# Four attention groups with a set-up each become one bulk projection and one loop of 16 sequences, and the transposed scores go one row group at a time

## What is computed

```python
x = x + tanh(g_xattn[0]) * L0_xattn(layernorm(x), ctx)   # 16 heads of 8 features, softmax over 120 keys, output projection
x = x + tanh(g_ffn[0])   * L0_ffn(layernorm(x))          # 16 experts, gates of the best 4 of each row, clipped sigmoid-gated units
x = x + tanh(g_xattn[1]) * L1_xattn(layernorm(x), ctx)   # one head of 128 features
x = x + tanh(g_ffn[1])   * L1_ffn(layernorm(x))          # 128 -> 512, 9 butterfly stages, gelu, 9 butterfly stages, 512 -> 128
```

## Time and profile before

| | us |
|---|---|
| three runs, median (lowest, highest) | 579.15 (575.86, 581.64) |
| the profiled execution, own time | 580.77 |
| its span, first to last instruction | 578.9 |
| PE busy | 448.4 (77%) |
| DVE busy | 354.1 (61%) |
| POOL busy | 264.3 (46%) |
| ACT busy | 226.5 (39%) |
| mean granted TensorE clock | 0.853 |

### The profile page before, as it was taken

How to read it: one execution, slowest core, us unless ns; L and a number is a source line. 1 busy time by engine, 2 the same in 40 slices (tenths; PEclk the granted TensorE clock), 3 DMA queues, 4 the chain that set the end, 5 groups by cost and what they waited for, 6 DMA issues and landing times. The chain is left out here.

```text
span 578.9 us, 8643 instructions
## 1 busy us (share of the span) xinstructions
PE 448.4 (77%) x2977; PEld 301.6 (52%) x2977; DVE 354.1 (61%) x849; ACT 226.5 (39%) x409; POOL 264.3 (46%) x286
## 2 busy tenths in 40 slices
PE   0347967885798579834999895999869998957785
PEld 0336746663676467623565453555445554524455
DVE  0755543562463346334779999789977998674321
ACT  1112321322123112323566764576537655725421
POOL 8999954980799552000334335234422434240000
PEclk9999976985986588655599998899969997997889
DMA  7112102200431220020000000000000000000001
GB/s 218 39 54 75 37 1 91 70 6 5 142 117 43 72 72 1 0 73 0 1 0 1 2 1 0 1 1 1 0 0 0 0 1 1 1 0 0 19 19 36
DMA packets 13440, 17.38 MB, mean 30 GB/s; under 512 B 1840, under 2 KB 9954, under 8 KB 13412
## 3 DMA queue, kind: packets, MB, share of 16 engines
q1 hardware_dynamic: 9804, 12.98, 7.0%
q10 hardware_dynamic: 3032, 1.96, 1.3%
q0 software_dynamic: 576, 2.10, 1.1%
HBM read 15.98 MB, written 1.05 MB: 29 GB/s over the span
## 5 line engine op out<-in xcount | busy, mean ns | idle before, releaser
L358 POOL TENSOR_TENSOR rings<-rings 128x512 f32<-128x512 f32 x32 | 42.3, 1322 | 98.7 <-DVE rings L1234 91.8
L771 PE MATMUL bank<-xhl,w_hi 128*128 128x512 f32 (+1 forms) x128 | 79.8, 624 | 0.0
L507 ACT ACTIVATE rings<-bank,b1c 128x512 f32<-128x512 f32 x64 | 44.1, 689 | 76.1 <-PE bank L773 45.6
L358 POOL TENSOR_TENSOR wide<-rings 128x512 f32<-128x512 f32 x32 | 41.7, 1304 | 58.6 <-DVE rings L1234 56.5
L1014 DVE TENSOR_REDUCE nt<-bank 128x4 f32<-128x480 f32 x64 | 37.6, 649 | 46.3 <-PE bank L647 46.3
L429 ACT ACTIVATE wide<-bank 120x512 f32<-120x512 f32 x64 | 33.0, 603 | 76.4 <-PE bank L668 76.4
L772 PE MATMUL bank<-xhl,w_lo 128*128 128x512 f32 (+1 forms) x128 | 53.6, 419 | 0.0
L773 PE MATMUL bank<-xhl,w_hi 128*128 128x512 f32 (+1 forms) x128 | 53.6, 418 | 0.0
L1227 DVE SCALAR_TENSOR_TENSOR rings<-rings,bank 128x512 f32<-128x512 f32 x64 | 43.6, 681 | 9.8 <-ACT rings L510 7.1
L1234 DVE TENSOR_TENSOR rings<-rings 128x512 f32<-128x512 f32 x64 | 44.3, 692 | 4.4 <-DVE rings L1230 0.2
L305 POOL TENSOR_TENSOR bft<-bw,bfly 128x256 f32<-128x256 f32 x34 | 29.9, 879 | 34.0 <-DMA bw<-in_L_ffn_down_weights 19.6
(11 more groups left out here) (226 smaller groups left out, 882.6 us busy)
## 6 DMA issues: line engine op xcount, KB each, us to landing
bw<-in_L_ffn_up_weights SPq DMA_DIRECT2D x9, 512.0 KB, 3.7
bw<-in_L_ffn_down_weights SPq DMA_DIRECT2D x9, 512.0 KB, 3.8
bw<-in_L_ffn_w POOLq DMA_DIRECT2D x4, 512.0 KB, 4.2
x_sb<-in_x SPq DMA_DIRECT2D x4, 256.0 KB, 5.3
out<-xr SPq DMA_DIRECT2D x4, 256.0 KB, 2.3
ctx_in<-in_ctx SPq DMA_DIRECT2D x4, 240.0 KB, 3.1
bfly<-in_L_ffn_W_exp ACTq DMA_DIRECT2D x1, 256.0 KB
wcon<-in_L_ffn_W_con ACTq DMA_DIRECT2D x1, 256.0 KB
```

What stands on the lines that cost most here:

```text
L358: pool.tensor_tensor(es[e % len(es)], ea[:, e % 2, :], ec[:, e % 2, :], ALU.mult).then_inc(s["m_s"], 1)
L507: act.activation(ea[:, e % 2, :], SB[1 + e % 2][:, :], ACT.Identity, bias=b1c[:, 0, e:e + 1]).then_inc(s["m_a"], 1)
L771: pe.matmul(bk[:, :], w1_hi[:, e, branch, :], low(g), start=True, stop=False)
```

## The change

Bulk part: all 16 contexts and all 16 sequences are projected before the first scores, in four groups, on ACT, PE and DVE. Keys and queries come out of one full matmul a group (`keys`, `queries`) with their bias added by ACT; to get them into the layout of row groups they are stored to DRAM by SP (`k_rows`, `q_rows`) and read back by four DMAs for keys and four for queries (`stack_k`, `stack_q`). Groups 0 and 1 are read back at once, 2 and 3 in the loop. The row of ones for the maxima is filled in advance. The values of both layers come from one matmul and stay in SBUF (v_all); ACT spreads those of one sequence into heads (`spread_values`).

Loop: one pipeline over b = 0 to 17, in which sequence b has its transposed scores, b + 1 its scores and maxima, b - 1 its values and b - 2 its output projection. `scores` keeps four banks for itself. `scores_t` has two banks (4 and 5) and is cut in four calls of one row group (four matmuls) each, with other work between; the third and fourth wait for the exponentials of the first and second. The values of b - 1 lie behind the third. The sums with the maxima go to a buffer of their own (qm).

Around it: no loop instruction is left, all groups are written out. The experts' first weights are split first on POOL, then the 9 up stages; the 9 down stages are cut into 27 parts, one behind the product of each of the experts 2 to 28 of the mixture. A stage is now two products of 128x512 (`straight`, `crossed`) and a sum, where it was four of 128x256 and a sum. PE's turning of the folded down weights and of the bias moves from ahead of the mixture to behind it. SP issues the load of the experts' second weights as soon as `xr` is made. The wider set-up of constants on POOL (`pick_e_raw`, `bst`, `wq_st`, `wk_st`) goes.

The diff, cut to its core:

```diff
+            for g in range(G):
+                sp.wait_ge(s["kt_rdy"], g + 1)
+                sp.dma_start(k_rows[:, g * GB * M:(g + 1) * GB * M], kt_row[:, :]).then_inc(s["k_stored"], 16)
+                sp.wait_ge(s["k_stored"], 16 * (g + 1))
+                if g < 2:
+                    stack_k(g)
+                sp.wait_ge(s["qt_rdy"], g + 1)
+                sp.dma_start(q_rows[:, g * GB * NT:(g + 1) * GB * NT], qt_row[:, :]).then_inc(s["q_stored"], 16)
+                sp.wait_ge(s["q_stored"], 16 * (g + 1))
+                if g < 2:
+                    stack_q(g)
+            sp.wait_ge(s["xr_rdy"], 1)
+            sp.dma_start(w2_sb[:, :, :], a["L0_ffn_w2"].rearrange("e i h -> i e h")).then_inc(s["ld_w2"], 16)
+            for g in range(2, G):
+                sp.wait_ge(s["st_mm"], (g - 1) * GB * HG)
+                stack_k(g)
+                stack_q(g)
...
+            def down_stage(k, part):
+                n = NQ + STAGES + k
+                w = bw[:, n % 2, :]
+                src = wdn[:, :, :].rearrange("p c d -> p (c d)") if k == 0 else bfly[:, k % 2, :]
+                if part == 0:
+                    fetched(n)
+                    straight(w, STAGES - 1 - k, src, P)
+                elif part == 1:
+                    crossed(w, STAGES - 1 - k, src, P, True)
+                else:
+                    summed(bfly[:, (k + 1) % 2, :], P)
+                    fetch(n + 2)
+                    if k == STAGES - 1:
+                        pool.tensor_copy(bft[0:1, 0:1], bfly[0:1, STAGES % 2, 0:1]).then_inc(s["bf_rdy"], 1)
...
+                    if 0 <= n < 3 * STAGES:
+                        down_stage(n // 3, n % 3)
                     if e == LAG + 2 and not first(g):
...
+            def spread_values(b):
+                act.wait_ge(s["v_rdy"], b // 2 + 1)
+                if b >= 2:
+                    act.wait_ge(s["pv_mm"], b - 1)
+                for i in range(2):
+                    ins = act.activation(
+                        vst[:, b % 2, :, :].rearrange("p (x i) c -> p x i c", i=2)[:, :, i, 16 * i:16 * i + HD],
+                        v_all[:, b, 0:D].rearrange("p (x i d) -> p x i d", i=2, d=HD)[:, :, i, :], ACT.Copy)
+                ins.then_inc(s["v_st"], 1)
+            def exps(b, gg):
+                n = b * HG + gg
+                act.wait_ge(s["st_mm"], n + 1)
+                act.activation(prob[b % 2][:, gg, :], ST[gg % 2][0:M, :], ACT.Exp, scale=SCALE).then_inc(s["exp_rdy"], 1)
+            def heads_out(b):
+                act.wait_ge(s["pv_mm"], b + 1)
+                act.activation(ot[:, :], PO[:, 0:2 * P], ACT.Copy).then_inc(s["ot_rdy"], 1)
+            def attn_t(b):
+                act.wait_ge(s["on_turned"], b + 1)
+                act.activation(ont[:, :], TP[:, 0:P], ACT.Copy).then_inc(s["ont_rdy"], 1)
+            act.wait_ge(s["consts"], 1)
+            spread_values(0)
+            for b in range(NB + 2):
+                if b < NB:
+                    exps(b, 0)
+                if 0 <= b - 2:
+                    attn_t(b - 2)
+                if b < NB:
+                    exps(b, 1)
+                if 0 <= b - 1 < NB:
+                    heads_out(b - 1)
+                if b < NB:
+                    exps(b, 2)
+                    exps(b, 3)
+                if b + 1 < NB:
+                    spread_values(b + 1)
...
+            def keys(g):
+                pe.wait_ge(s["ctx_rdy"], g + 1)
+                if g >= 1:
+                    pe.wait_ge(s["kt_rdy"], g)
+                pe.matmul(bank[4][:, 0:GB * M], wt[:, WK0, :], ctx_t[:, g % 2, :], start=True, stop=True).then_inc(s["k0_mm"], 1)
+                if g >= 1:
+                    pe.wait_ge(s["k1_rdy"], g)
+                pe.matmul(bank[5][:, 0:GB * M], wt[:, WK1, :], ctx_t[:, g % 2, :], start=True, stop=True).then_inc(s["k1_mm"], 1)
...
+            def queries(g):
+                pe.wait_ge(s["xnt_rdy"], g + 1)
+                if g >= 1:
+                    pe.wait_ge(s["qt_rdy"], g)
+                pe.matmul(bank[0][:, :], wt[:, WQ0, :], xnt[:, :], start=True, stop=True).then_inc(s["q_mm"], 1)
...
-            pe.wait_ge(s["w_rdy"], 1)
+            queries(G - 1)
+            pe.wait_ge(s["qt_rdy"], G)
             pe.wait_ge(s["b1_rdy"], 1)
             pe.wait_ge(s["wc_rdy"], 1)
...
-                def scores(u):
-                    pe.wait_ge(s["kx_rdy"], g * GB + u + 1)
-                    pe.wait_ge(s["qx_rdy"], g * GB + u + 1)
-                    for r in range(HR):
-                        for gg in range(HG):
-                            if r == 0:
-                                need(pe, "exp_rdy", (g * GB + u - 1) * HG + gg + 1 if u >= 1 else g * GB * HG)
-                            p0 = 32 * gg
-                            mm = pe.matmul(SB[gg][:, r * M:(r + 1) * M], qs[p0:p0 + 32, u % 2, r, :],
-                                           ks[p0:p0 + 32, u % 2, r, :], start=True, stop=True)
-                            if r == HR - 1:
-                                mm.then_inc(s["s_mm"], 1)
...
-                def scores_t(u):
-                    pe.wait_ge(s["ntq_rdy"], g * GB + u + 1)
-                    for r in range(HR):
-                        for gg in range(HG):
-                            p0 = 32 * gg
-                            mm = pe.matmul(SB[gg][0:M, r * P:(r + 1) * P], ks[p0:p0 + 32, u % 2, r, :],
-                                           qs[p0:p0 + 32, u % 2, r, :], start=True, stop=True)
-                            if r == HR - 1:
-                                mm.then_inc(s["st_mm"], 1)
...
-                def project(u):
-                    pe.wait_ge(s["ont_rdy"], g * GB + u + 1)
-                    pe.matmul(TP[:, P:2 * P], ont[:, :], wt[:, WO0, :], start=True, stop=True).then_inc(s["o_mm"], 1)
-                k_stack(0)
-                q_stack(0)
-                for u in range(-1, GB):
-                    if u + 1 < GB:
-                        scores(u + 1)
-                    if u >= 1:
-                        project(u - 1)
-                    if u >= 0:
-                        values(u)
-                    if u + 2 < GB:
-                        k_stack(u + 2)
-                    if u + 1 < GB:
-                        turn_max(u + 1)
-                    if u + 2 < GB:
-                        q_stack(u + 2)
-                    if u >= 0:
-                        turn_heads(u)
-                    if u + 1 < GB:
-                        scores_t(u + 1)
-                    if u >= 0:
-                        turn_attn(u)
...
+            def rows_of(b):
+                return (b // GB) % 2, slice(b % GB * M, (b % GB + 1) * M), slice(b % GB * P, (b % GB + 1) * P)
+            def scores(b):
+                i, mc, tc = rows_of(b)
+                if b % GB == 0:
+                    pe.wait_ge(s[f"ks_ld{i}"], 16 * HG * (b // (2 * GB) + 1))
+                    pe.wait_ge(s[f"qs_ld{i}"], 16 * HG * (b // (2 * GB) + 1))
+                need(pe, "nt_rdy", b)
+                for r in range(HR):
+                    for gg in range(HG):
+                        mm = pe.matmul(SB[gg][:, r * M:(r + 1) * M], qs[32 * gg:32 * gg + 32, i, r, tc],
+                                       ks[32 * gg:32 * gg + 32, i, r, mc], start=True, stop=True)
+                mm.then_inc(s["s_mm"], 1)
+            def turn_max(b):
+                pe.wait_ge(s["nt_rdy"], b + 1)
+                need(pe, "x1_rdy", b - 2)
+                pe.transpose(TP[:, 0:P], nt[:, :, :].rearrange("p g c -> p (g c)"), ident[:, :]).then_inc(s["nt_turned"], 1)
+            def scores_t(b, groups):
+                i, mc, tc = rows_of(b)
+                pe.wait_ge(s["ntq_rdy"], b + 1)
+                need(pe, "exp_rdy", b * HG + groups[-1] - 1)
+                for r in range(HR):
+                    for gg in groups:
+                        mm = pe.matmul(ST[gg % 2][0:M, r * P:(r + 1) * P], ks[32 * gg:32 * gg + 32, i, r, mc],
+                                       qm[32 * gg:32 * gg + 32, b % 2, r, :], start=True, stop=True)
+                        if r == HR - 1:
+                            mm.then_inc(s["st_mm"], 1)
+            def values(b):
+                pe.wait_ge(s["exp_rdy"], (b + 1) * HG)
+                pe.wait_ge(s["v_st"], b + 1)
+                need(pe, "on_rdy", b)
+                for half in range(2):
+                    for odd in range(2):
+                        for j in range(4):
+                            h = half * 8 + 2 * j + odd
+                            mm = pe.matmul(PO[32 * j:32 * j + 32, half * P:(half + 1) * P], vst[:, b % 2, h, :],
+                                           prob[b % 2][:, h % HG, (h // HG) * P:(h // HG + 1) * P],
+                                           start=(odd == 0), stop=(odd == 1))
+                mm.then_inc(s["pv_mm"], 1)
+            def turn_heads(b):
+                pe.wait_ge(s["ot_rdy"], b + 1)
+                for half in range(2):
```

(77 more changed lines are left out.)

656 lines of the change are left out of this document (285 added, 371 removed).

## The result

The changed kernel takes 617.2 us (median of 4 runs, 614.2 to 623.3) against 578.1 for the kernel before: 1.068 times as long, 95% interval 1.059 to 1.078. It is slower, where 544 was forecast with a range of 512 to 578. The profiled execution is the one of 614.23 us (span 612.4), 33.5 more than that of before.

A forecast was written before the change was run, and what follows sets the result against it. PE was taken to bound the attention, PE and DVE both near full in the mixture. Attention -59, between the stages -4.6 and mixture +28 gave -35.6 on 580.77, 545.2; less 1.6 to the median, rounded 544 us, range 512 to 578.

The forecast's parts named there:

- The bound: Attention loop: PE stays the bound, with the work and waits of DVE and ACT beside it.
- The loop at either clock: Attention loop: one sequence takes 7.3 us at 2.4 GHz, with groups 0 and 1 overlapping, and about 12.7 at 1.2 GHz.
- rival price of 8.1: Attention loop: if group 1 has to follow group 0, a sequence takes 8.1 us at 2.4 GHz instead of 7.3.
- The share of the clock: Attention loop: 26% of the time at half rate, kept from the old pipelined stretches, giving 8.3 us a sequence.
- both signs: Loop clock: no drain speaks for better; transposed scores on a quarter of the array for 3.5 us may speak for worse.
- Part 1: A sequence in the new loop: projections leave PE, transposed scores grow; period 8.3 us, bounds 7.3 and 10.5.
- Rival (d): Loop: clock stays at 0.5 for most of it, one row group of four in use; period 12.5, total 611; chance 0.1.
- The start: Bulk part: SP's chain of stores and read-backs puts the first scores at 48 us, bounds 43 and 56.
- The emptying: End of the attention loop: two emptying rounds, priced by the calls left in them at 7 us.
- Between attention and mixture: Before the mixture: the waits for PE's turning and the second weights go, minus 4.6 us.
- The mixture: Experts 2 to 28: POOL's 27 parts and DVE's SBUF operations exclude each other, plus 28 us; without L1234 plus 13.
- The rival at 5 to 10: Mixture: the lock costs only 5 to 10 us, period as forecast, total 521 to 527; chance 0.16.

The follow-up runs named there:

- the run with dense products: Changed kernel with one added product over all 128 rows and 512 columns ahead of each of the four single-row-group calls; 599.4 us.
- pairs: Changed kernel with transposed-score groups 0 and 1 in one call, 2 and 3 in another; four runs of 565.4, 566.4, 575.6 and 527.3 us.
- the old kernel with single groups: Kernel before, with only its transposed scores reordered so that row groups come one after another; 580.2 us, 1.0045 of the kernel before.
- all edits: Changed kernel with paired groups, loosened start and the second folding ahead of the mixture, no added product; six runs from 502.1 to 529.4 us.
- the start loosened: Changed kernel with two buffers each for K and Q rows, earlier stores, later read-backs, fewer waits for keys, first root earlier; 591.7 us.

## Why the prediction was wrong

**The bound: right. The loop at either clock: right in the number, by luck in part.** PE sets the pace, and the four exponentials, the sum and the maxima all lie beside it. A group alone takes 1.13 us at 2.4 GHz (1.15), and the period at 1.2 GHz is 12.51 (12.7). But the sum had group 1 free beside group 0, and it is not: 16 instructions take 2.92 us at 1.2 GHz, where full overlap is the pair's 2.06 and none is two calls of 2.06, so 0.9 us were missing in a sequence at half clock. What hid this is that the calls overlap at their edges: the rows of one sequence shown in the section on the result, from one L749 to the next, add up to 13.44 us and take 12.51. The 7.30 of the run with dense products is likewise not the sum's 7.3: there all four groups stand alone. By the old kernel's call of four groups (2.75 us, so (2.75 - 1.13) / 3 = 0.54 for each further group against 1.06 alone), the changed loop at 2.4 GHz would be about 6.8, an estimate. The prediction's rival price of 8.1, group 1 waiting in full, is further off.

**The share of the clock: the step that failed.** "I keep 26%" took the share at half rate from the four old stretches over to the new loop; measured, it is 100%. From 8.3 to 12.51 are 67 us on 16 sequences. I had named both signs, no drain for a better clock and a quarter of the array for a worse one, and gave the second 0.10. What I didn't weigh was what leaves the loop: the products over 128 rows, which stand in Part 1 as a gain of PE's time alone. Rival (d) is what happened: period 12.5 and 611 us forecast, 12.51 and 617 measured. Its reason, one row group of four in use, is half of the story: pairs stayed at 1.2 GHz for 130 us on two row groups, and the old kernel with single groups kept 0.80. That the rows in use matter is shown by the products over 128, 64 and 32 rows. That it was the leaving of the projections which tipped the loop is argued, not shown. How much work over all rows is enough isn't settled either: two products a sequence were enough with pairs in both loops that I read, and the eight times of those two kernels lie close together; one was enough in the loop that I read; with none, neither loop that I read (pairs alone, and all edits) was at 2.4 GHz from its start.

**The start: too small, beyond its bound.** First scores at 65.4 for 48, bounds 43 to 56. Queries(0)'s copy came at 34.0 instead of 27. The normed rows, turned, lay in SBUF at 26.8, but PE has the second group's keys, context and values ahead of queries(0) in its program:

```profile
26.24 0.60 ACT L468 ACTIVATE xnt<-bank 128x512 f32<-128x512 f32 x1 [1.56 <-PE bank L695]
31.97 1.02 PE L702 MATMUL bank<-xnt,wt 128*128 128x512 f32 x2
```

That order is 5 of the 7 us. The other 2 are left of the 3.5 by which keys(0)'s copy was late, as it waited until 19.96 for the last small load (16.5 forecast). From the first store of Q to the landing of Q2's, 34.7 to 63.3, it is 28.6 us for the forecast's 17.5. The five stores took 2.4, 5.4, 5.1, 5.1 and 2.5 us, 20.5 for 13.3: 7 us, priced by the 2.3 of the output's stores at the kernel's end. Between the stores lay 8.1 for the 4.2 of the read-backs: 4 us, as ACT has other copies between a K row and its Q row (43.94 and 45.97, 58.48 and 60.05). The three slow stores had 512 KB loads of POOL in flight with them; that these loads cause the slow landings wasn't tested alone. That the chain was there to be taken away is shown: with the start loosened the first scores come at 42.7, before the earliest bound.

**The emptying: right.** From the last turned maxima to the last residual it is one period and 7 us by the forecast, 19.5 at 12.51; measured 18.5 (251.8 to 270.4). Two of the first periods were shorter (7.9 and 11.2), 6 us less that I didn't have.

**Between attention and mixture: right**, -4.8 for -4.6.

**The mixture: right.** +23.9 for +28, DVE's means up as named, the window 126 for "near 130". The POOL product took 1.51 to 1.59 (1.6) and the sum 1.44 in there (1.31). The rival at 5 to 10 fell. The Trainium skill's page "SBUF — State Buffer", section on the two sides of SBUF, which was weighed for L1234, holds: that operation with two SBUF inputs grew most (+349 ns), and was rightly in the sum. (Without it the forecast's own sum gives plus 9, not the plus 13 stated.)

With the measured terms in the places of the forecast ones, the profiled execution is 545.2 + 67.4 (clock) + 17.4 (start) - 6 (first periods) + 0.8 (the old attention ended at 250.2, not 251) - 0.2 (between) - 4.1 (mixture) - 5.8 (the rest, not explained) = 614.7, against 614.2 measured.

## What to carry over

Before work is moved out of a loop, ask what it does for the clock: at equal busy time, loops with added matmuls over 32 or 64 rows left PE at 1.2 GHz and the same number over 128 rows brought it to 2.4, so that a loop with more work was faster. Row groups cost nothing beside each other, half or more of their price directly one after another, and all of it with other calls between, so order calls by how many banks let them run together, and look whether an engine behind them (here ACT) hides the difference anyway. Work on POOL beside DVE's SBUF operations makes these longer, and it counts where DVE is the limit: 25 us in the mixture, 12 on the chain of small operations before it, nothing in the attention loop. Where an engine's program is written by hand, look in its order for what stands ahead of the call that the next chain begins with.
